# A scratch fill with a wait behind every indirect DMA of GpSimd

## What is computed

```python
x = x + attn_a(layernorm(x), w_qkv, w_out, q_gain)     # causal, rotary
x = x + ffn(layernorm(x), router_w, ..., wg, wu, wd, swg, swu, swd)
x = x + attn_b(layernorm(x), Wqkv, Wproj, bproj)       # full
x = x + ffn(layernorm(x), router_w, ..., wg, wu, wd, swg, swu, swd)

def ffn(x, ...):                                       # 2048 tokens
    _, topk_idx = top_k(flat @ router_w + router_bias, 4)   # 4 of 64 experts
    comb = renormalised softmax scores at topk_idx
    routed = sum over experts e of comb[n, e] * (silu(flat @ wg[e]) * (flat @ wu[e])) @ wd[e]
    shared = (silu(flat @ swg) * (flat @ swu)) @ swd
    return routed + shared
```

## Time and profile before

| | before |
|---|---|
| median of 3 timed runs | 1205.18 us (1205.13 to 1210.4) |
| span of the profiled execution | 1217.2 us |
| busy: PE, DVE, ACT, POOL | 76%, 58%, 38%, 41% |
| indirect DMAs on POOL | 128 scatters (126.7 us busy), 128 gathers (97.0 and 32.5 us busy) |
| mean granted TensorE clock | 0.867 |

### The profile page before, as it was taken

One profiled execution on the slowest core, in us unless ns is written; L12 is line 12 of the kernel. 1 busy time (PEld: TensorE's weight loads), 2 busy tenths in 40 slices (PEclk: granted clock), 3 DMA queues, 4 the chain that ended last, 5 costly groups with the idle time before them and its releaser, 6 DMA issues. The chain is left out here.

```text
span 1217.2 us, 23699 instructions
## 1 busy us (share of the span) xinstructions
PE 920.7 (76%) x7450; PEld 692.7 (57%) x7450; DVE 706.3 (58%) x2262; ACT 465.0 (38%) x978; POOL 497.3 (41%) x575
## 2 busy tenths in 40 slices
PE   6987999988625979983586899997658298998430
PEld 5764666677514767862475455576536177786320
DVE  7879888665806334543365889757544633454243
ACT  3653565521000544651365578831101054564000
POOL 2002344364551323317471343448374332332756
PEclk9997999998767999997698799998767688999665
DMA  7496999299723798734259678209121479984434
GB/s 245 82 174 107 257 230 259 73 274 261 199 78 99 229 268 257 252 129 117 70 146 199 118 110 118 37 12 287 52 100 58 128 218 263 270 246 143 122 94 121
DMA packets 159162, 197.86 MB, mean 163 GB/s; under 512 B 17376, under 2 KB 137696, under 8 KB 155872
## 3 DMA queue, kind: packets, MB, share of 16 engines
q1 hardware_dynamic: 105920, 101.96, 36.9%
q0 software_dynamic: 22848, 68.18, 17.7%
q10 hardware_dynamic: 30272, 26.22, 7.2%
HBM read 132.86 MB, written 90.18 MB: 183 GB/s over the span
## 5 line engine op out<-in xcount | busy, mean ns | idle before, releaser
L944 ACT ACTIVATE tmp<-ps 128x256 f32<-128x256 f32 (+1 forms) x344 | 155.6, 477 | 130.7 <-PE ps L891 58.3
L525 POOL DMA_INDIRECT xd<-big,slot x128 | 126.7, 990 | 100.0 <-DVE slot L1511 62.3
L1074 ACT ACTIVATE tmp<-ps 128x384 f32<-128x384 f32 (+1 forms) x256 | 134.8, 543 | 61.8 <-PE ps L696 38.3
L564 POOL DMA_INDIRECT spill<-yd,slot x96 | 97.0, 1011 | 56.2 <-DVE X L1220 27.4
L477 POOL COPY arena<-negmax 24x2048 bf16<-24x2048 bf16 x32 | 60.5, 1890 | 134.2 <-ACT negmax L944 91.2
L605 PE MATMUL ps<-arena 96*128 96x256 bf16 (+1 forms) x512 | 96.9, 275 | 16.9 <-DVE tmp L1289 7.9
L634 PE MATMUL ps<-xt,weights 128*128 128x256 f32 x256 | 70.0, 434 | 45.6 <-issue 24.6
L693 PE MATMUL ps<-arena 120*128 120x256 bf16 (+1 forms) x512 | 100.6, 263 | 0.5 <-ACT tmp L1074 0.2
L1648 DVE SCALAR_TENSOR_TENSOR tmp<-tmp,ps 128x128 f32<-128x128 f32 x128 | 36.8, 287 | 101.4 <-ACT tmp L1143 101.0
L1116 ACT ACTIVATE tmp<-ps 128x512 f32<-128x512 f32 x24 | 14.2, 597 | 212.0 <-remote 120.5
L891 PE MATMUL ps<-ident,big 128*128 128x128 f32 x512 | 73.8, 289 | 21.1 <-DVEq L298 13.0
(11 more groups left out here) (198 smaller groups left out, 1988.6 us busy)
## 6 DMA issues: line engine op xcount, KB each, us to landing
big<-xd POOLq DMA_DIRECT2D x128, 256.0 KB, 4.7
arena<-parts SPq DMA_DIRECT2D x192, 128.0 KB, 5.4
xd<-zero SPq DMA_DIRECT2D x8, 2048.0 KB, 13.8
spill<-in_we SPq DMA_DIRECT2D x128, 128.0 KB, 3.1
yd<-tmp POOLq DMA_DIRECT2D x64, 256.0 KB, 3.1
yd<-tmp ACTq DMA_DIRECT2D x64, 256.0 KB, 3.5
arena<-in_we SPq DMA_DIRECT2D x8, 1024.0 KB
yd<-zero SPq DMA_DIRECT2D x8, 1024.0 KB
```

Source lines behind the costliest of these rows:

```text
L525: pool.indirect_dma_start(xd[:, :], bass.IndirectOffsetOnAxis(ap=slot[:, i, k:k + 1], axis=0), xn_all[:, i, :], None).then_inc(scattered.s ...
L564: pool.indirect_dma_start(gring[n % GRING], None, yd[:, :], bass.IndirectOffsetOnAxis(ap=slot[:, b * TB + m % TB, m // TB:m // TB + 1], ax ...
L944: return act.activation(dst, src, ACT.Copy)
L1074: act.activation(prob[h % 8][:, 0:n], ps[2 + h % 2][:, 0:n], ACT.Exp).then_inc(exp_ready.sem, 1)
```

## The change

Behind every indirect DMA, scatter and gather alike, GpSimd now fills a tile of its own, `pause_at`, 128 x 128 in f32 (64 KB), and waits for the semaphore that this fill counts up. Nothing reads the tile. The order of the DMAs, the slots and all other engines' programs stay as they are.

```diff
+        pause_at = sb("pause_at", [P, 128])
...
+        paused = signal("paused")
+        pauses = [0]
...
+            def pause():
+
+                pauses[0] += 1
+                pool.memset(pause_at[:, :], 0.0).then_inc(paused.sem, 1)
+                pool.wait_ge(paused.sem, pauses[0])
...
                         pool.indirect_dma_start(xd[:, :], bass.IndirectOffsetOnAxis(ap=slot[:, i, k:k + 1], axis=0),
                                                 xn_all[:, i, :], None).then_inc(scattered.sem, 16)
+                        pause()
...
                         pool.indirect_dma_start(gring[n % GRING], None, yd[:, :],
                                                 bass.IndirectOffsetOnAxis(ap=slot[:, b * TB + m % TB, m // TB:m // TB + 1], axis=0)
                                                 ).then_inc(g_in[n % GRING].sem, 16)
+                        pause()
```

## The result

| | before | after |
|---|---|---|
| median of the timed runs | 1205.16 us (1203.26 to 1210.4, 4 runs) | 1153.89 us (1148.97 to 1157.85, 4 runs) |
| ratio, 95% interval | | 0.9577 (0.9541 to 0.9613) |
| span of the profiled execution | 1217.2 us | 1156.3 us |
| busy: PE, DVE, ACT, POOL | 76%, 58%, 38%, 41% | 78%, 61%, 40%, 48% |
| mean granted TensorE clock | 0.867 | 0.894 |

The account below looks back on a forecast made before the run. Late TensorE updates during GpSimd's unbroken indirect DMAs were taken as the bound. Terms of -20, -20, -14 and +8 us gave -46, a span of 1171 us; with the median 12.0 below the span, 1159 us, range 1135 to 1228.

Parts of the forecast that it names:

- What bounds it: Routing stages and gathers: TensorE's updates come through late while GpSimd issues indirect DMAs without a break, up to 25.9 us.
- late by 2.6 us: Streams of indirect DMAs: with pauses, a late TensorE update is only as late as late in the first gather, 2.6 us.
- The price of a pause: Each indirect DMA step of GpSimd: grows by 0.25 us, from 1.26 to 1.51 us; bounds 0 and 1.32 us.
- Each held-up fill now breaks it: GpSimd's streams: a held-up fill stretches the step towards 2.58 us, TensorE's updates get through, the step falls back.
- B: The experiments' theory for GpSimd's streams that the length of the step matters; no size of its own.
- Most of it only after the stream's end: Streams of indirect DMAs: most of what TensorE reports comes through only once GpSimd's stream has ended.
- Rival 1: All streams: the pause doesn't let updates through, which still come at the stream's later end; +44 us, 1249 us; chance 0.24.
- The four terms: Routing of layers 0 and 1, gathers of layers 0 and 1: -20, -20, -14 and +8 us, sum -46 us.
- The reading by which a pause only costs: GpSimd's streams, by the Trainium skill: they could not hold TensorE up, so a pause would only cost; no size given.

Follow-up runs that it names:

- the one of one column: Fill cut to one column, with its wait, behind every indirect DMA except in layer 1's gather; 1174.18 us, 0.975 of the kernel before.
- the clear condition: Experiments beside which the kernel before took 1102.1 and 1101.5 us, not 1206.8 and 1201.7; no profile there has a wait that ends "remote".
- the kernel without the last pauses: The changed kernel without the pauses in the gather of layer 1; 1131.31 us beside 1101.47 us for the kernel before, ratio 1.027.
- set 3: Two kernels without pauses in layer 1's gather: one-column fill behind every other DMA, 1174.18 us; 128-column fill behind every eighth, 1217.67 us; kernel before 1201.68 us.
- every eighth: The changed kernel's fill and wait only behind every eighth indirect DMA, scatters and gathers alike; 1108.13 us beside 1102.1 us for the kernel before, ratio 1.007.
- the wait one late: Against the changed kernel, a fill of 248 columns, waited for only behind the next DMA; 1139.47 us beside 1101.47 us for the kernel before, ratio 1.035.
- 512 columns: The changed kernel with a fill of 512 columns instead of 128, with the wait; 1217.67 us, 1.011 of the kernel before.

## Why the prediction was right, and where not

**What bounds it: right, for the condition it was made in.** Late updates of TensorE set the length of the routing stages and of the first gather, the pause takes them away, and the time falls by 4.2%. Twice measured: 0.958 and 0.955. Where the forecast had "late by 2.6 us" the reader starts 0.03 us after the group; the one update still late is so by 2.5 us.

**The price of a pause: right.** 0.20 us for a forecast of 0.25. The fill is 0.22 us as read from the two other fills; the wait behind it costs 0.11 us beside a fill that nobody waits for, but the 0.30 us ahead of the next DMA were there anyway.

**"Each held-up fill now breaks it": wrong.** I expected the fill's own update to be held up, the step to grow towards 2.58 us, and this to let TensorE's updates through. The fills are never held up, neither in the changed kernel nor in the one of one column, where TensorE's update was 10.6 us late at the same time. Seven steps in the second routing stage have 0.53 to 1.09 us instead of 0.28 ahead of the DMA, but seven of the same lengths stand there in the clear condition too. Timeline of POOL, the longest of them in the changed kernel:

```profile
877.58 0.96 POOL L535 DMA_INDIRECT xd<-big,slot  x1 [1.09 <-issue]
```

and in the kernel without the last pauses, in the clear condition:

```profile
879.37 0.97 POOL L535 DMA_INDIRECT xd<-big,slot  x1 [1.09 <-issue]
```

What fits the runs in its place is B: the more time a step takes, the less is late. By step, the waits that end "remote" at the tanh of the routing stages are 120.5 and 126.2 us at 1.26, 138.1 at a mean of 1.28, 88.8 and 70.9 at 1.35, none at 1.46 and at 1.79; VectorE's one late update at 1.46 is gone at 1.79. The steps stay even; it is the pace of the whole stream that matters, and a single break of 0.5 us every eight DMAs does nothing. That the length alone suffices at 1.46 us, with no DMA waiting for a fill, was run only in the clear condition, so it isn't shown; nor is it excluded that the wait adds a part (set 3).

**"Most of it only after the stream's end": not in two of the five cases.** The reader of the group that ended at 888.14 started at 914.04, and the stream ran on. Timeline of POOL, before:

```profile
915.67 0.96 POOL L525 DMA_INDIRECT xd<-big,slot  x1 [0.30 <-issue]
930.30 0.96 POOL L525 DMA_INDIRECT xd<-big,slot  x1 [13.67 <-DVE slot L1511]
```

In the first gather the late copy starts at 582.49 and the stream runs until 592.81. So updates came through in the middle of an unbroken stream; what released them just then, no run shows.

**Rival 1** had the same view of a pause as too short to let anything through, with the point of decision "from some step over 1.51 us on". The mechanism is close to what was found; the point lies between 1.35 and 1.46 us, at most 0.1 us under what the change makes. The forecast's sign rested on a margin that no row of before showed: that the pause is long enough was luck.

**The four terms.** Against the same set's kernel before (131.9, 136.2, 125.8, 94.7 us) the changed kernel again (111.4, 108.9, 112.6, 102.0) has -20.5, -27.3, -13.2 and +7.3 for a forecast of -20, -20, -14 and +8. Against the first profile it is -31.8, -28.9, -13.6 and +6.0. That profile was 12 us above its median, and its routing stage of layer 0 was 12.5 us longer than in the second; the forecast took the terms from it and then subtracted the 12 us from the result, and the two errors met. Of the routing stage of layer 0, forecast at 374 - 249.8 = 124.2 us and measured at 112.6, 4.2 us are the landing (5.2 us from the last scatter to the first matmul, not 9.4) and 7.4 GpSimd's stream: the pause was 0.05 us cheaper, and the 9.63 us for the third group's slots, which I had taken as a wait that stays, are gone: they were themselves made by late updates, since VectorE's slots need TensorE's ranks (at that place 0.30 us with every eighth in the clear condition). Of that of layer 1, forecast at 117 us and measured at 108.2, 4.2 us are again the landing and 5 the stream: its second group waited 5.1 us for slots, not 11. The other stages grew by 7 us together, which no term had.

**Why it was nearly wrong.** None of my cases had the condition itself as a variable. In the clear condition the kernel before takes 1102 us and the pause costs 3.5% (with the wait one late). The trace of before showed that updates were late; it could not show that the same program on another occasion has none of it.

**The reading by which a pause only costs.** SBUF — State Buffer, section Who interferes with whom, of the Trainium skill, says that PE and ACT never wait on anyone. By that the change could only cost; in the clear condition all kernels with a pause agree with it (1.007 to 1.035), in the late one the changed kernel doesn't (0.958 and 0.955). It speaks of SBUF's ports, and what is late here is an update of a semaphore.

## What to carry to other kernels

If a trace shows "remote" waits for TensorE inside a stream of GpSimd's indirect DMAs, with TensorE itself slowed by "issue", slow the whole stream a little (here from 1.26 to 1.46 us a step); a break now and then doesn't help, and every further 0.1 us costs. But first profile the same kernel on another occasion and, if you can, another chip: where nothing is late, the same pause is a pure loss, and no version here is faster than before in both conditions. Before a wait counts as cover for an added cost, ask whether the wait isn't a result of the very thing that the change removes.

## What the runs showed of the hardware that was not expected

- The same program takes 1202 to 1207 us or 1101 to 1102 us, depending on the chip or the occasion. The four sets ran on four chips, two in each condition. Only the stretches with indirect DMAs differ. How long transfers take doesn't: the median landing of the expert's rows is 4.7 us in the first profile and 4.9 us in that of every eighth in the clear condition, and the packets of GpSimd's queue took 17.7% of a span of 1217.2 us and 19.2% of 1112.5, 215 and 214 us. What makes the condition (the chip, or what ran beside) is open.
- The traces themselves follow the condition. They keep 17,158 and 17,079 records of semaphore updates for the kernel before, 19,161 and 19,117 for the changed one and 20,687 with 512 columns, but 21,312 to 21,672 in every profile of the clear condition. Where more is late, more records are missing; whether the recording has a part in the lateness isn't shown.
- The late updates are those that other engines wait for from TensorE, and some of VectorE (1.07 us in the earlier trace rows). GpSimd's own updates came through within its 0.28 us, but for seven steps of a routing stage and one of each gather (0.53 to 1.09 us), as long in the clear condition.
- A fill behind an indirect DMA runs in line also when nobody waits for it. 0.17 us stand between it and the next DMA, 0.28 if that waits for it, and 0.30 between two DMAs that follow each other.
- Half the rows make an indirect DMA hardly shorter for GpSimd: 0.89 us for 64 rows, 0.96 for 128.
